# Loading all raw weights at once, splitting them ahead of the jobs, and moving three gathers and five loads

## The chip, the cores and the metric

The kernel runs on one core of one Trainium2 chip. The metric is the device time of one execution in microseconds. The kernel before took 1120.15 us (median of three runs, 1119.07 to 1122.03). The profiled execution took 1120.02 us, of which the profile's span covers 1118.3 us.

## The reference, cut to what matters

For each of 512 samples, 39 table rows of 16 values are gathered, giving x with shape (batch, 39, 16). Three layers (CIN layers) follow, and then a small tower:

```
e = stack([tbl_f[ids[:, f]] for f in 0..38], axis=1)       # (512, 39, 16)
prev = x = e
for k in 0, 1, 2:                                          # 39 or 128 rows in prev, 128 units out
    z = einsum('bmd,bhd->bdmh', x, prev)                   # outer product over fields
    t = einsum('bdc,co->bdo', z, w[k]) + b[k]              # w0: 39*39 x 128, w1, w2: 39*128 x 128
    t = transpose(t); t = t / sqrt(sum(t * t over units and d))
    logit.append(t); prev = t
features = sum(concatenate(logit), axis=-1)                # then dense_ctx, W_top1, W_top2, W_top3
```

All is float32. The raw weights w1 and w2 of layers 1 and 2 are 128 x 39 x 128 values each (2.5 MB).

## The kernel before

**Tiling.** The batch is cut into 16 chunks of 32 samples, 512 columns (sample, d) each. Layers 1 and 2 are computed as *jobs*: a job (k, c, q) is layer k, chunk c and one quarter (128 columns). An iteration `it` holds four jobs of layer 1 for chunk it, and then four jobs of layer 2 for chunk it - 1. So jobs 0 to 3 are layer 1 of chunk 0, jobs 4 to 7 layer 1 of chunk 1, jobs 8 to 11 layer 2 of chunk 0, and so on: 128 jobs.

**A job** has 10 banks of up to four fields. For each bank TensorE does three matmuls (lines 533 to 535): low part of prev by high weights, high prev by low weights, high by high. This is how float32 accuracy is had from the rounded f32r type; it needs each raw weight split in a high part (`split_high`, a copy on ScalarE, line 406) and a low part (`split_low`, a subtraction of two tiles in SBUF on VectorE, line 690). Five banks (`bank_a`, ring of two) are scaled by x on ScalarE (`scale_bank`, L423) and added up on GpSimd (`add_bank`, L307). The other five (`bank_d`, ring of three) are scaled and added on VectorE (`add_field`, L723), which begins when the four GpSimd adds of its job are done; `merge` (L742) folds the parts. TensorE takes D and A banks in turn (places 0 to 9 of a job), and its A banks run seven banks ahead of the job (LEAD). The last D bank of a job has three fields and so 384 columns, which marks the end of a job in the trace (place 8).

**Layer 0** of chunk c is done in pairs of fields. The gathered rows go through DRAM: GpSimd gathers chunk c in ten indirect DMAs (`gather`, L295) into one of two buffers; SyncE waits for them, stores them in `x_scratch` (`store_chunk`, L355 to 359), waits for the store and loads them back, copied and shifted, as `x_pairs` (`load_pairs`, L368 and L374; 14 DMAs in four groups p = 0 to 3). VectorE multiplies each group (`make_pairs`, L701, two tiles of SBUF in), TensorE sums tile by tile (`pair_matmul`, L598, 7 tiles). Then `finish` (L447, L450), `norms`, `roots`, `reciprocal_step`, `make_prev` (L788), `high` (L463, ScalarE) and `low` (L312, GpSimd) give the two parts of prev for the next layer.

**Order written out by hand.** Each engine executes one fixed list. GpSimd: the gathers of chunk 0, two constants (`ones`, `identity`), the gathers of chunk 1, `low(1, 0)`, the adds of seven banks, and then for each job its five adds with gathers of chunk it + 2 between them: three a job in iteration 0 (jobs 0 to 2, the tenth in job 3), two a job later. `start_chunk(c)` comes before the first gather of a chunk: it waits until chunk c - 1 has been gathered and chunk c - 2 stored, and makes the row numbers of chunk c + 1 (L280). VectorE has the pairs of chunk 2 at fields 2 and 12 of job 4, 12 of job 5 and 5 of job 6; TensorE sums the first tile after place 5 of job 4.

**The weights before.** ScalarE's queue loads w0a and w0b, the biases, and then w1 in three parts, each of which is issued when the one before has landed (L471 to 473). They are split at once, before the pairs of chunk 0. The raw w2 comes in six parts (`W2_PARTS`): the first is loaded after chunk 0's pairs, and in each of jobs 0 to 5 ScalarE splits one and issues the next (L489 to 494), and VectorE splits its low part behind field 18 (L834). The low w2 is wanted by the first layer 2 bank, seven banks ahead of job 8.

Of the kernel before, what the change touches and what calls it, by code (L numbers as in the profile page):

```python
# [123 lines left out]
W2_PARTS = [(0, 7), (7, 14), (14, 21), (21, 27), (27, 33), (33, 39)]  # L124
W1_PARTS = [(0, 16), (16, 28), (28, 39)]
# [5 lines left out]
def cin_kernel(nc, idx_in, base_in, table, ctx_t, w0a, w0b, w1, w2, b0, b1, b2,  # L131
# [7 lines left out]
    with ExitStack() as ctx:  # L139
# [73 lines left out]
        w_loaded = {k: sem(f"w{k}_loaded") for k in (1, 2)}  # L213
# [47 lines left out]
        def x_of(c, q, m):  # L261
            return x_col[:, c % 3, q, m:m + 1]

# [14 lines left out]
        def _(pool):  # L278
# [48 lines left out]
            for j in range(GATHERS):  # L327
                gather(1, j)
            low(1, 0)
            for at in range(LEAD):  # L330
                add_bank(at)
            for n in range(NJ):
                k, c, q = JOBS[n]
                it, place = (c, q) if k == 1 else (c + 1, q + TILES)

                per_step = 3 if it == 0 else 2
                first = place * per_step if it + 2 < CHUNKS else GATHERS
                if it + 2 < CHUNKS and place == 0:
                    start_chunk(it + 2)
                for a in range(A_BANKS):  # L340
                    add_bank(A_BANKS * n + LEAD + a)
                    if 1 <= a <= per_step and first + a - 1 < GATHERS:
                        gather(it + 2, first + a - 1)
                    for item, at in HALVES_AT.items():
                        if at == (n, a):
                            low(*item)

        @block.sync
        def _(sp):
# [12 lines left out]
            def load_pairs(c, p):  # L362
                rows = scratch[c, :, :].rearrange("(m b) e -> m (b e)", b=CB)
                tiles = PAIR_GROUPS[p]
                for kk in range(PER_TILE):
                    at = slice(kk * FIELDS, (kk + 1) * FIELDS)
                    if p == 0:
                        sp.dma_start(x_rep[at, :], rows[0:FIELDS, :]).then_inc(pairs_loaded[p], 16)  # L368
                    offsets = [PAIR_OFFSETS[PER_TILE * i + kk] for i in tiles if PER_TILE * i + kk < OFFSETS]
                    if offsets:  # L370
                        first = rows[offsets[0]:offsets[0] + FIELDS, :]
                        window = bass.AP(first.tensor, first.offset,
                                         [[ROWS, FIELDS], [PER_TILE * ROWS, len(offsets)], [1, ROWS]])
                        sp.dma_start(x_rot[at, tiles[0]:tiles[0] + len(offsets), :],  # L374
                                     window).then_inc(pairs_loaded[p], 16)

# [3 lines left out]
            for c in range(CHUNKS):  # L380
# [4 lines left out]
                for p in range(NP):  # L385
                    load_pairs(c, p)
                if c + 1 < CHUNKS:
                    store_chunk(c + 1)
                if c == 2:

                    sp.wait_ge(w_lo_made[1], len(W1_PARTS))
                    sp.wait_ge(w_lo_made[2], len(W2_PARTS))
# [10 lines left out]
        def _(act):  # L403
            def split_high(k, part, lo, hi):
                act.wait_ge(w_loaded[k], 16 * (part + 1))
                nc.scalar.activation(w_hi[k][:, lo:hi, :], w_raw[k][:, lo:hi, :], ACT.Copy).then_inc(w_hi_made[k], 1)
# [58 lines left out]

            act.dma_start(w0_sb[0:PAIR_ROWS, :, :], w0a).then_inc(w0_loaded, 16)
# [13 lines left out]
            act.dma_start(w_raw[2][:, 0:W2_PARTS[0][1], :], w2[:, 0:W2_PARTS[0][1], :]).then_inc(w_loaded[2], 16)  # L480
# [44 lines left out]
        def _(pe):  # L525
# [11 lines left out]
            def bank_for_act(at):  # L537
# [4 lines left out]
                if n == 0:  # L542
                    m = a * PER_BANK
                    pe.wait_ge(w_lo_made[1], 1 + sum(m >= lo for lo, _ in W1_PARTS[1:]))
                if (k, c, q) == (2, 0, 0) and a == 0:
                    pe.wait_ge(w_lo_made[2], len(W2_PARTS))
# [6 lines left out]
            def bank_for_dve(n, d):  # L553
                k, c, q = JOBS[n]
                at = D_BANKS * n + d
                if n == 0:
                    pe.wait_ge(w_lo_made[1], len(W1_PARTS))
# [129 lines left out]
        def _(dve):  # L687
            def split_low(k, part, lo, hi):
                dve.wait_ge(w_hi_made[k], part + 1)
# [118 lines left out]
            features(0)  # L808
            for n in range(NJ):
                for u in range(D_FIELDS):  # L810
# [23 lines left out]
                    if u == 18 and n < len(W2_PARTS):  # L834
                        split_low(2, n, *W2_PARTS[n])
# [65 lines left out]
```

## Time and profile before

| | |
|---|---|
| median of three runs | 1120.15 us |
| profiled execution, its span | 1120.02 us, 1118.3 us |
| TensorE (PE) busy | 1049.8 us, 94% |
| VectorE (DVE) busy | 939.6 us, 84% |
| GpSimd (POOL) busy | 900.5 us, 81% |
| ScalarE (ACT) busy | 814.0 us, 73% |
| mean granted TensorE clock | 0.989 |
| moved by DMA | 41.18 MB |

Times are microseconds from the start of the span. An engine's busy share is over the whole span, so it says nothing on a single stage: stages are read from the timeline (what ran when), the windows (busy time, clock and DMA in a stretch) and the chain of waits (what the end of the program hung on, step by step). SP is SyncE, which only issues DMAs; SPq and ACTq are DMA issues of those engines. "issue" is time in which an engine waited for nothing that the profile shows.

### The profile page before, as it was taken

The page shows a single profiled execution, that of the slowest core. Times are in us where ns is not written, and L with a number is a line of the kernel's source. Part 1 is how long each engine was busy: PE and PEld are TensorE (multiplying, and loading weights), DVE is VectorE, ACT ScalarE, POOL GpSimd, SP SyncE. Part 2 cuts the span into 40 slices and gives each one's busy share as a digit, 9 for nine tenths or more (in the row PEclk, how much of TensorE's full clock was granted, in tenths as well). Part 3 has the DMA queues.
Part 4 walks back from the last instruction along what each step waited for, and adds up shares of the span by engine and source line. Part 5 has one row for each costly group of instructions (what it writes and reads, how often), then busy time and mean ns, then how long its engine had stood idle before and what let it go on. Part 6 is the DMA issues. An engine that isn't in the chain of part 4 may idle for free.

```text
span 1118.3 us, 17869 instructions
## 1 busy us (share of the span) xinstructions
PE 1049.8 (94%) x4376; PEld 788.5 (71%) x4376; DVE 939.6 (84%) x3189; ACT 814.0 (73%) x2756; POOL 900.5 (81%) x726
## 2 busy tenths in 40 slices
PE   0696999999999999999999999999999999999999
PEld 0364677777777777777777777777777777778773
DVE  2285789899889989899998989999898998898892
ACT  2464587877878787787868777786878778788872
POOL 6586698888989888888988888888888888677770
PEclk9898999999999999999999999999999999999999
DMA  5513022020203002030302102020300203000000
GB/s 157 131 48 100 2 74 51 7 68 3 71 3 72 3 7 67 3 71 3 72 3 46 29 4 71 3 71 3 66 8 8 66 3 72 1 1 1 1 1 0
DMA packets 57166, 41.18 MB, mean 37 GB/s; under 512 B 37963, under 2 KB 40907, under 8 KB 56934
## 3 DMA queue, kind: packets, MB, share of 16 engines
q1 hardware_dynamic: 49522, 32.81, 12.2%
q10 hardware_dynamic: 2420, 5.96, 1.7%
q0 software_dynamic: 5120, 1.29, 1.5%
q8 instruction: 34, 0.56, 0.2%
q14 instruction: 70, 0.57, 0.2%
HBM read 38.09 MB, written 1.94 MB: 36 GB/s over the span
## 4 chain that ended last, share of the span: by engine, by line
PE 58%; POOL 26%; ACT 7%; issue 5%; DMA 2%; DVE 1%; SPq 1%; POOLq 0%; ACTq 0%; DVEq 0%
POOL sums L307 20%; PE acc L598 9%; PE bank_a L533 9%; PE bank_a L535 8%; PE bank_a L534 8%; PE bank_d L533 7%; PE bank_d L535 7%; PE bank_d L534 7%; POOL gathered L295 5%; ACT scaled L423 5%; ACT t L447 1%; DMA x_pairs<-x_scratch 1%; ACT squares L450 1%; PE turned L574 1%; PE bank_a L652 1%
## 5 line engine op out<-in xcount | busy, mean ns | idle before, releaser
L307 POOL TENSOR_TENSOR sums<-sums,scaled 128x512 f32<-128x512 f32 x512 | 686.7, 1342 | 141.8 <-ACT scaled L423 107.3
L723 DVE SCALAR_TENSOR_TENSOR sums<-bank_d,x_col,sums 128x128 f32<-128x128 f32 x2176 | 626.5, 339 | 108.8 <-PE bank_d L535 66.4
L423 ACT ACTIVATE scaled<-bank_a,x_col 128x128 f32<-128x128 f32 x2048 | 585.9, 382 | 153.0 <-PE bank_a L535 146.4
L533 PE MATMUL bank_a<-w_hi,prev_lo 128*128 128x512 f32 x640 | 283.1, 442 | 21.1 <-ACT scaled L423 8.9
L533 PE MATMUL bank_d<-w_hi,prev_lo 128*128 128x512 f32 (+1 forms) x640 | 278.0, 434 | 5.5 <-DVE sums L742 5.4
L535 PE MATMUL bank_a<-w_hi,prev_hi 128*128 128x512 f32 x640 | 254.4, 398 | 0.0
L534 PE MATMUL bank_a<-w_lo,prev_hi 128*128 128x512 f32 x640 | 253.8, 396 | 0.0
L535 PE MATMUL bank_d<-w_hi,prev_hi 128*128 128x512 f32 (+1 forms) x640 | 245.6, 384 | 0.0
L534 PE MATMUL bank_d<-w_lo,prev_hi 128*128 128x512 f32 (+1 forms) x640 | 245.4, 383 | 0.0
L423 ACT ACTIVATE sums<-bank_a,x_col 128x128 f32<-128x128 f32 x512 | 146.7, 372 | 70.5 <-PE bank_a L535 70.5
L295 POOL DMA_INDIRECT gathered<-in_table,idx x160 | 169.4, 1059 | 30.9 <-issue 19.2
L533 PEld LDWEIGHTS bank_a<-w_hi,prev_lo 128*128 128x128 f32 x640 | 121.1, 189 | 71.2 <-ACT scaled L423 23.6
L533 PEld LDWEIGHTS bank_d<-w_hi,prev_lo 128*128 128x128 f32 x640 | 121.0, 189 | 54.2 <-DVE sums L723 12.3
L534 PEld LDWEIGHTS bank_a<-w_lo,prev_hi 128*128 128x128 f32 x640 | 121.6, 190 | 33.4 <-issue 13.7
L534 PEld LDWEIGHTS bank_d<-w_lo,prev_hi 128*128 128x128 f32 x640 | 121.4, 190 | 30.2 <-issue 11.1
L535 PEld LDWEIGHTS bank_a<-w_hi,prev_hi 128*128 128x128 f32 x640 | 121.2, 189 | 29.1
L535 PEld LDWEIGHTS bank_d<-w_hi,prev_hi 128*128 128x128 f32 x640 | 120.6, 188 | 22.2
L598 PE MATMUL acc<-z,w_sb 117*128 117x512 f32 (+1 forms) x224 | 116.2, 606 | 7.6 <-DVE z L701 7.0
L701 DVE TENSOR_TENSOR z<-x_pairs 117x1024 f32<-117x1024 f32 x64 | 101.9, 1594 | 14.4 <-DMA x_pairs<-x_scratch 14.4
L723 DVE SCALAR_TENSOR_TENSOR bank_d<-bank_d,x_col,sums 128x128 f32<-128x128 f32 x256 | 78.0, 348 | 10.2 <-PE bank_d L535 8.2
L742 DVE TENSOR_TENSOR sums<-bank_d,sums 128x128 f32<-128x128 f32 x256 | 71.2, 278 | 0.0
L598 PEld LDWEIGHTS acc<-z,w_sb 117*128 117x128 f32 (+1 forms) x224 | 42.1, 195 | 20.3 <-issue 13.5
(57 smaller groups left out, 470.5 us busy)
## 6 DMA issues: line engine op xcount, KB each, us to landing
x_pairs<-x_scratch SPq DMA_DIRECT2D x144, 156.0 KB
x_pairs<-x_scratch SPq DMA_DIRECT2D x80, 78.0 KB
gathered<-in_table,idx POOLq DMA_INDIRECT x160
w_raw<-in_w ACTq DMA_DIRECT2D x3, 448.0 KB
x_scratch<-gathered SPq DMA_DIRECT2D x16, 72.0 KB, 2.2
w_raw<-in_w ACTq DMA_DIRECT2D x3, 384.0 KB
w_raw<-in_w ACTq DMA_DIRECT2D x1, 1024.0 KB
w_raw<-in_w ACTq DMA_DIRECT2D x1, 768.0 KB
```

The costliest lines, as they stand in the source:

```text
L295: nc.gpsimd.indirect_dma_start(out=gathered[0:n, c % 2, j, :], out_offset=None, in_=table[:, :], in_offset=bass.IndirectOffsetOnAxis(ap=id ...
L307: nc.gpsimd.tensor_tensor(out=sums[:, n % SUMS, :, :], in0=sums[:, n % SUMS, :, :], in1=scaled[:, a - 1, :, :], op=ALU.add).then_inc(a_add ...
L423: op = nc.scalar.activation(to[:, i, :], bank_a[at % A_RING][:, i * UNITS:(i + 1) * UNITS], ACT.Copy, scale=x_of(c, q, a * PER_BANK + i))
L447: nc.scalar.activation(t[:, k, :], ps[:, :], ACT.Identity, bias=bias[:, k:k + 1]).then_inc(biased, 1)
L450: nc.scalar.activation(squares[:, :], ps[:, :], ACT.Square, bias=bias[:, k:k + 1]).then_inc(squared, 1)
L533: nc.tensor.matmul(to, lo, w_h, start=True, stop=False)
L534: nc.tensor.matmul(to, hi, w_l, start=False, stop=False)
L535: return nc.tensor.matmul(to, hi, w_h, start=False, stop=True)
L598: mm = nc.tensor.matmul(acc0[:, :], w0_sb[0:rows, tile, :], z0[0:rows, tile, :], start=(tile == 0), stop=(tile == PAIR_TILES - 1))
L701: nc.vector.tensor_tensor(out=z0[0:rows, tiles[0]:tiles[0] + count, :], in0=x_rep[0:rows, :].unsqueeze(1).to_broadcast([rows, count, ROWS] ...
L723: nc.vector.scalar_tensor_tensor(out=taken(n, u) if u in LEFT else total, in0=taken(n, u), scalar=x_of(c, q, A_FIELDS + u), in1=total, op0 ...
L742: nc.vector.tensor_tensor(out=out, in0=in0, in1=in1, op=ALU.add).then_inc(merged, 1)
```

## The change

`W_LOADS` are three DMAs a layer; `W_PIECES` are the parts in which they are split, as before. ScalarE's queue now issues w1 (three DMAs) ahead of w0a and w0b, then the biases, then w2 (three DMAs) and the small ones of the tower, with no wait between. ScalarE splits all of w1 and three pieces of w2, waits for the store of chunk 0, issues the pair loads of groups 1 and 3 of chunk 0 itself (SyncE issues groups 0 and 2), and splits the other three pieces. VectorE waits for `ones`, so until GpSimd has issued chunk 0's gathers, splits w1 and three pieces of w2, makes chunk 0's pairs, splits piece 3, does the norm of chunk 0, waits for `low(1, 0)` and splits pieces 4 and 5. The splits in jobs 0 to 5 are gone. GpSimd starts chunk 2 ahead of `low(1, 0)`: row numbers and three gathers; the seven others are three a job in jobs 0 and 1 and one in job 2.

```diff
-W2_PARTS = [(0, 7), (7, 14), (14, 21), (21, 27), (27, 33), (33, 39)]
-W1_PARTS = [(0, 16), (16, 28), (28, 39)]
+W_LOADS = {1: [(0, 16), (16, 28), (28, 39)], 2: [(0, 14), (14, 27), (27, 39)]}
+W_PIECES = {1: [(0, 16), (16, 28), (28, 39)], 2: [(0, 7), (7, 14), (14, 21), (21, 27), (27, 33), (33, 39)]}
+GATHERS_BEFORE = 3
+W2_FIRST, W2_SECOND = 3, 4
+SP_GROUPS, ACT_GROUPS = [0, 2], [1, 3]
...
             for j in range(GATHERS):
                 gather(1, j)
+            start_chunk(2)
+            for j in range(GATHERS_BEFORE):
+                gather(2, j)
             low(1, 0)
...
                 first = place * per_step if it + 2 < CHUNKS else GATHERS
-                if it + 2 < CHUNKS and place == 0:
+                if it == 0:
+                    first += GATHERS_BEFORE
+                elif it + 2 < CHUNKS and place == 0:
                     start_chunk(it + 2)
...
-                for p in range(NP):
-                    load_pairs(c, p)
+                for p in range(NP) if c else SP_GROUPS:
+                    load_pairs(sp, c, p)
...
+            def load_raw(k):
+                for part, (lo, hi) in enumerate(W_LOADS[k]):
+                    act.dma_start(w_raw[k][:, lo:hi, :], raws[k][:, lo:hi, :]).then_inc(w_loaded[k][part], 16)
+
+            load_raw(1)
             act.dma_start(w0_sb[0:PAIR_ROWS, :, :], w0a).then_inc(w0_loaded, 16)
             act.dma_start(w0b_sb[0:PAIR_ROWS, :, :], w0b).then_inc(w0_loaded, 16)
             for k, b in enumerate((b0, b1, b2)):
                 act.dma_start(bias[:, k:k + 1], b).then_inc(bias_loaded, 16)
-            for part, (lo, hi) in enumerate(W1_PARTS):
-                if part:
-                    act.wait_ge(w_loaded[1], 16 * part)
-                act.dma_start(w_raw[1][:, lo:hi, :], w1[:, lo:hi, :]).then_inc(w_loaded[1], 16)
-            for part, (lo, hi) in enumerate(W1_PARTS):
-                split_high(1, part, lo, hi)
-            act.wait_ge(pairs_loaded[NP - 1], PAIR_LOADS[NP - 1] * 16)
+            load_raw(2)
             act.dma_start(top3_sb[:, :], w_top3).then_inc(top_bias_loaded, 16)
...
-            act.dma_start(w_raw[2][:, 0:W2_PARTS[0][1], :], w2[:, 0:W2_PARTS[0][1], :]).then_inc(w_loaded[2], 16)
+            for piece in range(len(W_PIECES[1])):
+                split_high(1, piece)
+            for piece in range(W2_FIRST):
+                split_high(2, piece)
+            act.wait_ge(scratch_stored, 48)
+            for p in ACT_GROUPS:
+                load_pairs(act, 0, p)
+            for piece in range(W2_FIRST, len(W_PIECES[2])):
+                split_high(2, piece)
...
             for n in range(NJ):
-                if n < len(W2_PARTS):
-                    lo, hi = W2_PARTS[n]
-                    split_high(2, n, lo, hi)
-                    if n + 1 < len(W2_PARTS):
-                        lo, hi = W2_PARTS[n + 1]
-                        act.dma_start(w_raw[2][:, lo:hi, :], w2[:, lo:hi, :]).then_inc(w_loaded[2], 16)
...
-            for part, (lo, hi) in enumerate(W1_PARTS):
-                split_low(1, part, lo, hi)
+            dve.wait_ge(ones_made, 1)
+            for piece in range(len(W_PIECES[1])):
+                split_low(1, piece)
+            for piece in range(W2_FIRST):
+                split_low(2, piece)
             for p in range(NP):
                 make_pairs(0, p)
+            for piece in range(W2_FIRST, W2_SECOND):
+                split_low(2, piece)
             sum_values(0, 0)
...
             features(0)
+            dve.wait_ge(prev_lo_made[1], 1)
+            for piece in range(W2_SECOND, len(W_PIECES[2])):
+                split_low(2, piece)
             for n in range(NJ):
...
-                    if u == 18 and n < len(W2_PARTS):
-                        split_low(2, n, *W2_PARTS[n])
```

## Rows read from the trace of the kernel before

**Rows 1.** The page: shares of the chain of waits, by engine.
```profile
PE 58%; POOL 26%; ACT 7%; issue 5%; DMA 2%; DVE 1%; SPq 1%; POOLq 0%; ACTq 0%; DVEq 0%
```

**Rows 2.** Timeline of TensorE, 384-column banks: jobs 3, 4, 11, 12, 20.
```profile
91.45 0.34 PE L533 MATMUL bank_d<-w_hi,prev_lo 128*128 128x384 f32 x1
...
113.55 0.34 PE L533 MATMUL bank_d<-w_hi,prev_lo 128*128 128x384 f32 x1
...
173.70 0.34 PE L533 MATMUL bank_d<-w_hi,prev_lo 128*128 128x384 f32 x1
...
181.48 0.34 PE L533 MATMUL bank_d<-w_hi,prev_lo 128*128 128x384 f32 x1
...
245.55 0.34 PE L533 MATMUL bank_d<-w_hi,prev_lo 128*128 128x384 f32 x1
```

**Rows 3.** Chain of waits around 100 us: start, length, what.
```profile
96.64 2.38 DMA gathered<-in_table,idx
...
100.10 1.92 DMA x_scratch<-gathered
...
104.04 4.26 DMA x_pairs<-x_scratch
...
109.70 2.05 PE acc L598 x2
```

**Rows 4.** Chain of waits from the start to the first job.
```profile
1.28 4.22 DMA base_sb<-in_bases
...
17.64 2.74 DMA gathered<-in_table,idx
...
25.45 3.65 DMA x_pairs<-x_scratch
...
30.93 7.96 PE acc L598 x14
...
44.24 1.27 POOL prev_lo L312
```

**Rows 5.** Timeline of GpSimd: row numbers, gathers of chunks 1 and 2.
```profile
20.46 1.51 POOL L280 TENSOR_TENSOR idx<-ids_sb,base_sb 128x10 int32<-128x10 int32 x1 [1.30 <-DMA gathered<-in_table,idx]
22.14 2.34 POOL L295 DMA_INDIRECT gathered<-in_table,idx  x1 [0.17 <-issue]
...
37.29 0.92 POOL L295 DMA_INDIRECT gathered<-in_table,idx  x1 [0.30 <-issue]
...
84.67 0.96 POOL L295 DMA_INDIRECT gathered<-in_table,idx  x1
...
90.82 0.96 POOL L295 DMA_INDIRECT gathered<-in_table,idx  x1 [2.07 <-issue]
```

**Rows 6.** Timeline of VectorE: splits of w1, its first add, splits in jobs.
```profile
19.61 5.50 DVE L690 TENSOR_TENSOR w_lo<-w_raw,w_hi 128x2048 fp32r<-128x2048 f32 x3 [12.19 <-ACT w_hi L406]
...
55.74 0.61 DVE L723 SCALAR_TENSOR_TENSOR sums<-bank_d,x_col,sums 128x128 f32<-128x128 f32 x2 [12.13 <-POOL sums L307]
...
66.80 1.07 DVE L690 TENSOR_TENSOR w_lo<-w_raw,w_hi 128x896 fp32r<-128x896 f32 x1
...
93.35 2.01 DVE L690 TENSOR_TENSOR w_lo<-w_raw,w_hi 128x768 fp32r<-128x768 f32 x1
```

**Rows 7.** Windows: last three columns are TensorE clock, DMA share, GB/s.
```profile
8.00:10.00 2.00, 0.00 (x0) 0.00 (x0) 0.00 (x0) 0.00 (x0) 1.55 (x2) 1.00 0.80 329
...
28.00:30.00 2.00, 0.32 (x4) 0.35 (x4) 0.43 (x1) 0.00 (x0) 1.39 (x3) 1.00 0.95 209
...
134.00:138.00 4.00, 4.00 (x12) 2.87 (x12) 1.26 (x5) 1.14 (x4) 1.72 (x2) 0.65 0.03 2
```

**Rows 8.** Chain of waits in job 6.
```profile
131.39 2.25 issue
133.64 0.76 PE bank_a L533
```

More of the change, by code:

```diff
@@ L212, in cin_kernel @@
         bias_loaded = sem("bias_loaded")
-        w_loaded = {k: sem(f"w{k}_loaded") for k in (1, 2)}
+        w_loaded = {k: [sem(f"w{k}_loaded{part}") for part in range(len(W_LOADS[k]))] for k in (1, 2)}
         w_hi_made = {k: sem(f"w{k}_hi_made") for k in (1, 2)}
@@ L262, in x_of, with load_pairs @@
             return x_col[:, c % 3, q, m:m + 1]
+        def load_pairs(queue, c, p):
+            rows = scratch[c, :, :].rearrange("(m b) e -> m (b e)", b=CB)
+            tiles = PAIR_GROUPS[p]
+            for kk in range(PER_TILE):
+                at = slice(kk * FIELDS, (kk + 1) * FIELDS)
+                if p == 0:
+                    queue.dma_start(x_rep[at, :], rows[0:FIELDS, :]).then_inc(pairs_loaded[p], 16)
+                offsets = [PAIR_OFFSETS[PER_TILE * i + kk] for i in tiles if PER_TILE * i + kk < OFFSETS]
+                if offsets:
+                    first = rows[offsets[0]:offsets[0] + FIELDS, :]
+                    window = bass.AP(first.tensor, first.offset,
+                                     [[ROWS, FIELDS], [PER_TILE * ROWS, len(offsets)], [1, ROWS]])
+                    queue.dma_start(x_rot[at, tiles[0]:tiles[0] + len(offsets), :],
+                                    window).then_inc(pairs_loaded[p], 16)
         def bdim(ap):
@@ L360, in store_chunk @@
                              g[:, 0:5, :]).then_inc(scratch_stored, 16)
[L362 to L375, printed above, removed]
             sp.dma_start(ids_sb[:, :], idx_in).then_inc(ids_loaded, 16)
@@ L389, in _ @@
                 if c == 2:
-                    sp.wait_ge(w_lo_made[1], len(W1_PARTS))
-                    sp.wait_ge(w_lo_made[2], len(W2_PARTS))
+                    sp.wait_ge(w_lo_made[1], len(W_PIECES[1]))
+                    sp.wait_ge(w_lo_made[2], len(W_PIECES[2]))
                     sp.dma_start(top1c_sb, w_top1[3 * 128:3 * 128 + EMB, :]).then_inc(top_loaded, 16)
@@ L403, in _, with split_high @@
         def _(act):
-            def split_high(k, part, lo, hi):
-                act.wait_ge(w_loaded[k], 16 * (part + 1))
+            def split_high(k, piece):
+                lo, hi = W_PIECES[k][piece]
+                part = [first <= lo < last for first, last in W_LOADS[k]].index(True)
+                act.wait_ge(w_loaded[k][part], 16)
                 nc.scalar.activation(w_hi[k][:, lo:hi, :], w_raw[k][:, lo:hi, :], ACT.Copy).then_inc(w_hi_made[k], 1)
@@ L543, in bank_for_act @@
                     m = a * PER_BANK
-                    pe.wait_ge(w_lo_made[1], 1 + sum(m >= lo for lo, _ in W1_PARTS[1:]))
+                    pe.wait_ge(w_lo_made[1], 1 + sum(m >= lo for lo, _ in W_PIECES[1][1:]))
                 if (k, c, q) == (2, 0, 0) and a == 0:
-                    pe.wait_ge(w_lo_made[2], len(W2_PARTS))
+                    pe.wait_ge(w_lo_made[2], len(W_PIECES[2]))
                 if q == 0 and a == 0:
@@ L687, in _, with split_low @@
         def _(dve):
-            def split_low(k, part, lo, hi):
-                dve.wait_ge(w_hi_made[k], part + 1)
+            def split_low(k, piece):
+                lo, hi = W_PIECES[k][piece]
+                dve.wait_ge(w_hi_made[k], piece + 1)
                 nc.vector.tensor_tensor(out=w_lo[k][:, lo:hi, :], in0=w_raw[k][:, lo:hi, :],
```

3 lines of the change are left out of this document (2 added, 1 removed).

## The prediction

> **What bounds the kernel now.** I read first the page's chain: its end hangs on TensorE for 58% and on GpSimd for 26% [rows 1], so over most of the span matmuls and adds hand over to each other. The change touches none of that. The 384-column banks on TensorE's timeline mark the jobs: from job 12 to job 20 they are 245.55 - 181.48 = 64.07 us apart [rows 2], and the same distance repeats, with one of 64.8, to the end. What is gained or lost ahead of job 12 should stand unchanged in the total, so I look only at the first 180 us.
>
> Two things there are longer than in the repeating part. From job 3 to job 4 the banks are 113.55 - 91.45 = 22.1 us apart, where the like step from job 11 to job 12 takes 7.78 [rows 2]. From job 4 to job 12 it is 67.93 us, 3.9 more than 64.07. The chain of waits says what the first gap is: the tenth gather of chunk 2, its landing, the store, the load of the first pairs, and the matmuls behind them [rows 3]. The second is in job 6, where TensorE waits 2.25 us for the low part of layer 2's first prev and then runs slowly [rows 8]. The chain from the start to the first job [rows 4] is the third place: 44 us in which row numbers, chunk 0's gathers, store, loads, 14 matmuls and the norm follow each other. There a delay counts in full.
>
> **Part 1: three gathers ahead of the first job (chunk 2 ready earlier).** The last gather of chunk 2 moves from job 3 (96.64 us) to the place in job 2 that now holds its seventh (84.67) [rows 3, 5]. Ahead of this place nothing is removed from GpSimd's list but one making of row numbers, at a time when TensorE is the bound; only some collision with VectorE's splits goes, some 0.3 us. So it is issued at 84.4 on the old clock. From the issue of the last gather to TensorE's first pair matmul it takes 109.70 - 96.64 = 13.1 us now [rows 3]: TensorE would have it at 97.5. When does TensorE want it? Job 3's last bank is at 91.45; I take 0.5 us off, for the VectorE splits and the gathers that no longer stand in jobs 2 and 3 (a split of 2.01 us at 93.35 [rows 6], and three gathers, one of them with 2.07 us idle ahead of it [rows 5], in the stretch where GpSimd was the bound). TensorE then comes to place 5 of job 4 at about 96.4 and waits 1.1 us. Job 4's last bank: 91.45 - 0.5 + 7.8 + 1.1 = 99.85, against 113.55: **-13.7 us**. Bounds: without any wait 14.8; if GpSimd reaches the gather 3 us later than I think, because it becomes the bound in jobs 0 and 1, 10.7.
>
> **Part 2: the splits leave jobs 0 to 5.** On VectorE six of 1.07 to 2.01 us [rows 6], on ScalarE six. In jobs 0 to 3 they lie beside TensorE or GpSimd and are in part 1. In job 5 one of about 1 us stands ahead of the norm of layer 1's first chunk, on which TensorE waits in job 6. Without it prev and its low part come about 0.7 us sooner, so the wait of 2.25 [rows 8] becomes 1.5. After this wait the granted clock falls (0.65 over 134 to 138 us, a mix of the two levels 1.2 and 2.4 GHz [rows 7]), and the first matmul takes 0.76 [rows 8]. If the clock holds after the shorter wait, the missing 0.35 of 4 us come back, 1.4. I count 0.7 and half of 1.4: **-1.4 us**; bounds -0.3 and -3.
>
> **Part 3: w1 first in the queue (row numbers later).** The ids and bases wait now 4.22 us for landing [rows 4], with w0 being loaded beside them. After the change 1 MB of w1 goes first, in rows of 8 KB for 3.5 KB, and w2 behind it. The trace doesn't show a small load beside so large rows. Lower bound 0 (the small rows are first in a queue of their own); upper bound: the wait doubles, 4.2. The nearest row is the last gather of chunk 0, which lands 2.74 after its start with w1's third part in flight, against 2.38 with nearly nothing [rows 4, 3]: small packets beside bulk lose 0.4 a time. Two loads in a row: I take **+1.0**, range 0 to 4.
>
> In all 5.96 MB now stand in one queue. At the 329 GB/s of 8 to 10 us [rows 7] they are in after 18 us, near 20 us, before the store; at 209 GB/s [rows 7] after 28.5 us, near 30, in the middle of the pair loads. I take the first, as its rows are the weights' own.
>
> w0 is now behind w1, so its two additions on VectorE fall among chunk 0's gathers: **+0.2**. The rest of VectorE's work waits for `ones`.
>
> **Part 4: two queues for chunk 0's pairs.** TensorE's 14 matmuls run from 30.93 for 7.96 us with no hole [rows 4]: they hang on group 0 alone, and what groups 1 and 3 gain is worth nothing. But the DMA engines are 95% busy from 28 to 30 us [rows 7], and group 0 (three loads of 78 KB, three of 156 KB, 0.7 MB) now shares them with 0.47 MB of group 1, issued beside it. At 209 GB/s that is 2.2 us if group 1 were all in front, and 0 if its loads fill holes of the issue. I take a third: **+0.7**, range -0.3 to 2.2. The Trainium skill, "DMA: Bandwidth & Descriptors", section "Issuing engines are not separate DMA queues", speaks against this part as well: DMAs of several issuers run on the same 16 engines, and only issue time is saved. By it the part brings nothing where the load is bound by the engines; if issue were the bound (six issues ahead of the landing in [rows 4]), it would neither help nor harm group 0.
>
> **Part 5: GpSimd ahead of the first job.** VectorE's splits lengthen GpSimd's instructions. While w1 was split (19.61 to 25.11 [rows 6]) the making of row numbers took 1.51 and a gather 2.34, where a gather alone takes 0.92 [rows 5]. With the short 1.15 of the next gather the loss was about 2.9 us in 4.65 us of overlap, 0.6 us a us. Now the splits run from about 18.8 for 5.5 + 3 x 1.07 = 8.7 us, to 27.5: 2.4 us more overlap, +1.5 us. Piece 3, in the last gathers, gives +0.6. Chunk 1's last gather then starts at 37.29 + 2.1 = 39.4, and lands 2.3 later, at 41.7. Only then may chunk 2 start: 0.4 for row numbers and start, three gathers at 1.25 with the 0.30 between them, 3.8: about 46.0. `low(1, 0)`, which started at 44.24 with its input ready [rows 4], stands behind them in GpSimd's list, and TensorE's first job waits for it. That is 1.8 late, of which 0.7 is already in part 4 (the gathers don't wait for the pairs): **+1.1**. Bounds: 0 if the overlap costs nothing more, 3.5 if each us of VectorE's splits costs a full one. The two pieces that VectorE splits behind `low` fit in the 12.13 us that it idles before the first job's adds [rows 6].
>
> For the overlap the Trainium skill has a rule: "SBUF — State Buffer", section "Who interferes with whom", says that a tensor_tensor with both inputs in SBUF and a GpSimd instruction that reads SBUF exclude each other, the second waiting for the whole first one. By that each split would cost its full length where GpSimd has work, and part 5 would be about +2.5 for +1.1. The rows show 0.6, as GpSimd can slip in between two splits.
>
> **Sum.** -13.7 - 1.4 + 1.0 + 0.2 + 0.7 + 1.1 = -12.1 us. The profiled execution took 1120.02, the median of the runs is 1120.15, so both are the same base: 1120.1 - 12.1 = 1108.0.
>
> **Rivals.**
> *A, the start eats more of it.* The bulk loads run at 209 GB/s and last to 30 us. Chunk 0's pair loads and w2's last 1.5 MB share the engines (+4 for group 0), ScalarE gets to its pair loads only when 5.2 MB are in, so groups 1 and 3 are late (+1), ids lose 2 to 3. For it: the only row with the DMA engines full shows 209 GB/s. Against: that row is of 2 KB pieces, the one with 329 of weights [rows 7]. Time: 1108.0 + 7 = 1115.0.
> *B, the gap closes wholly and the start costs nothing.* Ids, groups and `low` as before, no wait in job 4, clock kept in job 6: -14.8 - 2.1 - 0.3 = 17.2 less, 1102.9. For it: each of the costs is in parts not shown by the trace. Against: GpSimd's list must be 1.8 us longer by rows.
> *C, the gap is there all the same.* Chunk 2's loads wait for something else than the tenth gather. SyncE's list for it has only the pairs and the transpose of chunk 1, made in job 0. With the gap left and the start worse by 3: 1123; with the gap half closed, 1116. Against: the chain names each step [rows 3].
> *D, slower: the repeating part gets longer.* With another distance between the engines at job 12, the hand-over of matmuls and adds could settle on a longer period. It has one place and one price: with 13.5 iterations to go, 64.07 must become over 65.0 to eat 12 us; with 65.3 the time is 1124. For it: TensorE and GpSimd share the chain, so a shift between them can matter. Against: the period in the trace is reached after a start with a hole of over 10 us, so it doesn't look as if it hung on the start.
>
> **Chances.** The forecast (1104.5 to 1111.5) 0.66, A 0.14, B 0.10, C 0.05 (half of it slower), D 0.05, of which most is slower. I expect to tell 0.3%, 3.4 us, from no change. Faster: forecast, A, B and a little of C, 0.92; same: 0.03; slower: 0.05. The range for 8 in 10: 1103.0 to 1114.0, which takes in half of A and of B.
>
> **What the profile after would show.** Right: the 384-column bank of job 4 about 8.5 us behind that of job 3; the tenth gather of chunk 2 near 87 us; `low(1, 0)` starting near 47, right behind a gather; ids landing 1 us later; the wait in job 6 at or under 1.5 us, and 64.07 us between jobs 12 and 20. Wrong: group 0's first product before 29.6 (part 4 has the wrong sign), w2 in flight beyond 25 us (A), over 3 us of wait for pairs in job 4 (part 1), a period other than 64.07 (D). The forecast fails most easily at the start: the three unseen costs there sum to 2.9, and could be 0 or 8.

## The result, and the profile after

The changed kernel takes 1113.95 us (median of six runs, 1113.52 to 1115.38), the kernel before beside it 1120.91: ratio 0.994, 95% interval 0.9928 to 0.9953. The forecast was 12.1 us less; it became 7.0 by the medians (6.7 by the ratio). The direction was right and the size little more than half; 1113.95 is at the upper end of the range of 1103.0 to 1114.0. The two profiled spans differ by 1118.3 - 1112.3 = 6.0 us, and the ledger below is made for them.

First TensorE's timeline, the 384-column banks of jobs 0 to 4, 12 and 20, which answer to [rows 2]:

```profile
69.90 0.74 PE L550 MATMUL bank_d<-w_hi,prev_lo 128*128 128x384 f32 x1
80.58 0.34 PE L550 MATMUL bank_d<-w_hi,prev_lo 128*128 128x384 f32 x1
91.80 0.53 PE L550 MATMUL bank_d<-w_hi,prev_lo 128*128 128x384 f32 x1
100.22 0.34 PE L550 MATMUL bank_d<-w_hi,prev_lo 128*128 128x384 f32 x1
107.98 0.34 PE L550 MATMUL bank_d<-w_hi,prev_lo 128*128 128x384 f32 x1
...
175.76 0.34 PE L550 MATMUL bank_d<-w_hi,prev_lo 128*128 128x384 f32 x1
...
239.78 0.34 PE L550 MATMUL bank_d<-w_hi,prev_lo 128*128 128x384 f32 x1
```

The gap is gone: from job 3 to job 4 are 7.76 us for 22.1, and the repeating part is unchanged (239.78 - 175.76 = 64.02 for 64.07). But job 3 ends 8.77 us later than before (100.22 for 91.45), where I had expected 2.5. Job by job the lateness is 6.2 us in jobs 0 and 1 (their banks stood at 63.73 and 74.43 before), 7.7 in job 2 and 8.8 in job 3. Job 2 before the change, with the wait ahead of it:

```profile
83.34 0.50 PE L533 MATMUL bank_a<-w_hi,prev_lo 128*128 128x512 f32 x1 [1.87 <-POOL prev_lo L312]
...
84.14 0.35 PE L533 MATMUL bank_d<-w_hi,prev_lo 128*128 128x384 f32 x1
```

The chain from the start shows where the 6.2 come from; it answers to [rows 4]:

```profile
23.59 0.39 SPq L382
...
24.66 1.94 DMA x_scratch<-gathered
...
28.65 7.05 DMA x_pairs<-x_scratch
...
37.09 7.97 PE acc L615 x14
...
50.40 1.27 POOL prev_lo L334
```

The store of chunk 0 is issued at 23.59, where it was at 20.40 before: 3.2 late. The last load of group 0 takes 7.05 for 3.65 us, and the first pair matmul comes at 37.09 for 30.93, 6.16 late. From there on to `low(1, 0)` (50.40 for 44.24) nothing is added: the early gathers end before it. GpSimd's timeline, which answers to [rows 5], says when row numbers and gathers came:

```profile
8.87 0.48 POOL L302 TENSOR_TENSOR idx<-ids_sb,base_sb 128x10 int32<-128x10 int32 x2 [8.35 <-DMA base_sb<-in_bases]
...
47.23 0.94 POOL L317 DMA_INDIRECT gathered<-in_table,idx  x1 [0.30 <-issue]
50.40 1.26 POOL L334 TENSOR_TENSOR prev_lo<-prev,prev_hi 128x512 fp32r<-128x512 f32 x1 [2.22 <-ACT prev_hi L477]
...
86.04 0.96 POOL L317 DMA_INDIRECT gathered<-in_table,idx  x1 [2.13 <-issue]
87.02 2.67 POOL L329 TENSOR_TENSOR sums<-sums,scaled 128x512 f32<-128x512 f32 x2
89.65 1.26 POOL L334 TENSOR_TENSOR prev_lo<-prev,prev_hi 128x512 fp32r<-128x512 f32 x1
...
92.30 0.92 POOL L317 DMA_INDIRECT gathered<-in_table,idx  x1
```

The bases land at 8.8 and not at 5.5 us. In job 1 the ninth gather of chunk 2 (the program's 29th) has 2.13 us of idle ahead of it, and behind it in the list stands `low(1, 1)`, the low part for chunk 1, which TensorE wants in job 2 already, as its A banks run seven ahead. This idle was in the old trace too, at the same gather [rows 5], but there it was in job 2, with `low(1, 1)` already done. TensorE's timeline and the windows (last columns: granted clock, DMA share, GB/s) show what follows:

```profile
90.97 0.50 PE L550 MATMUL bank_a<-w_hi,prev_lo 128*128 128x512 f32 x1 [4.00 <-POOL prev_lo L334]
```

```profile
4.00:6.00 2.00, 0.00 (x0) 0.00 (x0) 0.00 (x0) 0.00 (x0) 0.00 (x0) 1.00 1.03 418
6.00:8.00 2.00, 0.00 (x0) 0.00 (x0) 0.00 (x0) 0.00 (x0) 0.00 (x0) 1.00 0.99 399
...
34.00:36.00 2.00, 0.17 (x2) 0.20 (x3) 0.28 (x1) 0.00 (x0) 1.39 (x3) 1.00 0.88 195
...
92.00:96.00 4.00, 4.00 (x13) 3.37 (x13) 1.82 (x8) 2.28 (x8) 2.87 (x4) 0.61 0.13 13
129.00:131.00 2.00, 2.00 (x5) 0.96 (x4) 1.26 (x5) 0.91 (x4) 0.96 (x1) 0.57 0.05 4
```

TensorE waits 4.00 us for that low part, where it waited 1.87 before. Over 92 to 96 us, behind this wait, the granted clock is 0.61, a mix of 2.4 and 1.2 GHz: some 3 us of it are at the lower level. The raw weights fill the DMA engines from 4 to 12 us, with up to 418 GB/s, and are in by about 21 us.

The ledger, in us of the profiled executions: start +6.2, jobs 2 and 3 +2.6, gap -14.3, job 4 to job 12 -0.15, the rest -0.3, sum -6.0. The forecast had, in the same places, +3.0, -0.5, -13.2, -1.4 and 0.

### The profile page after: what moved, and what is told of

The parts are those of the page before. It is cut to its first block, busy times and chain, and to the rows that moved or that the text cites. A ratio compares the mean times of both kernels' runs of the same rounds, so it can differ in the third digit from the quotient of the medians.

```text
span 1112.3 us, 17868 instructions
## 1 busy us (share of the span) xinstructions
PE 1047.5 (94%) x4376; PEld 788.4 (71%) x4376; DVE 939.0 (84%) x3189; ACT 812.8 (73%) x2756; POOL 900.9 (81%) x726
## 3 DMA queue, kind: packets, MB, share of 16 engines
q1 hardware_dynamic: 49145, 32.17, 12.1%
## 4 chain that ended last, share of the span: by engine, by line
PE 58%; POOL 27%; issue 7%; ACT 7%; DMA 1%; DVE 1%; SPq 0%; POOLq 0%; ACTq 0%; DVEq 0%
POOL sums L329 22%; PE acc L615 9%; PE bank_a L550 9%; PE bank_a L552 8%; PE bank_a L551 8%; PE bank_d L550 7%; PE bank_d L551 7%; PE bank_d L552 7%; POOL gathered L317 5%; ACT scaled L437 5%; ACT t L461 1%; PE turned L591 1%; PE bank_a L669 1%; DMA x_pairs<-x_scratch 1%; ACT squares L464 1%
## 5 line engine op out<-in xcount | busy, mean ns | idle before, releaser
L317 POOL DMA_INDIRECT gathered<-in_table,idx x160 | 168.7, 1054 | 31.3 <-issue 19.6
```

The costliest lines, as they stand in the source:

```text
L317: nc.gpsimd.indirect_dma_start(out=gathered[0:n, c % 2, j, :], out_offset=None, in_=table[:, :], in_offset=bass.IndirectOffsetOnAxis(ap=id ...
```

## The experiments

Theory: three things cost what the gap gave. (1) The 6 MB of bulk in one queue delay whatever is small and on the chain: ids, then the landing of chunk 0's gathers. (2) Group 0 of the pair loads shares the DMA engines with groups 1 and 3. (3) Gathers moved forward stand ahead of `low(1, 1)`. The rival to each stands in the expectation. All ratios are against the kernel before on the same chip. The kernels did not all run on one chip, and the kernel before took between 1120.9 and 1121.7 us beside them, so two kernels of the table are compared by their ratios; where the intervals overlap, as those of one_queue and the changed kernel just do, the difference of the times alone does not tell.

| kernel | median us | ratio (95% interval) |
|---|---|---|
| changed | 1113.95 | 0.994 (0.9928 to 0.9953) |
| one_queue | 1112.01 | 0.9914 (0.9898 to 0.9931) |
| ids_first | 1113.45 | 0.9926 (0.9908 to 0.9945) |
| no_early_gathers | 1125.74 | 1.0037 (1.0024 to 1.005) |
| before_gathers | 1112.03 | 0.9913 (0.9896 to 0.9929) |
| three_two_two | 1114.2 | 0.9933 (0.9917 to 0.995) |
| w2_behind | 1108.01 | 0.9879 (0.9862 to 0.9895) |
| before_gathers_ids | 1112.41 | 0.992 (0.9903 to 0.9936) |
| w0_first | 1114.03 (one run) | |
| behind_low | 1111.09 | 0.9912 (0.9897 to 0.9928) |
| six_early | 1107.4 | 0.9872 (0.9857 to 0.9887) |
| w2_behind_chunk1 | 1106.09 | 0.9859 (0.9844 to 0.9874) |
| all_moved | 1102.93 | 0.9832 (0.9819 to 0.9845) |

**The gap: no_early_gathers and before_gathers.**

```diff
-GATHERS_BEFORE = 3
+GATHERS_BEFORE = 0
```

> All ten gathers of chunk 2 are in the jobs again (three, three, three, one); the row numbers are still made ahead of the first job. Theory (the gap in job 4 hangs on the tenth gather): the step from the last bank of job 3 to that of job 4 goes from 7.76 back to about 22, jobs 2 and 3 lose their 2.6 us of delay, time 1114 + 14.3 - 2.6 = 1125.5, so slower than before the change. Rival (the removed splits closed the gap): the step stays under 12 and the time under 1118.

Jobs 3 and 4 on TensorE's timeline of this kernel:

```profile
97.30 0.34 PE L550 MATMUL bank_d<-w_hi,prev_lo 128*128 128x384 f32 x1
118.78 0.52 PE L550 MATMUL bank_d<-w_hi,prev_lo 128*128 128x384 f32 x1
```

The gap is back (21.48 us), and the time is 1125.74, slower than before the change. So the removed splits did not close it, and all of the change but the three gathers is a loss of 0.4%, with the interval clear of 1. Jobs 2 and 3 take 16.3 us here for 19.6 in the changed kernel: their delay comes with the gathers too. The 29th gather has its idle here as well (2.26 us), but behind `low(1, 1)`.

The other way round, the gathers alone in the kernel before:

```diff
                 gather(1, j)
+            start_chunk(2)
+            for j in range(3):
+                gather(2, j)
             low(1, 0)
...
-                if it + 2 < CHUNKS and place == 0:
+                if it == 0:
+                    first += 3
+                elif it + 2 < CHUNKS and place == 0:
                     start_chunk(it + 2)
```

> The kernel before the change with only the gathers moved (three of chunk 2 ahead of the first job, seven in jobs 0 to 2); weights, splits and queues as before. Theory (the gathers alone close the gap, all else of the change costs about 6 us at the start): first job at 45.7 to 46.5 as before, gap gone but for 1 us, time 1107 to 1110, faster than the changed kernel. Rival (the splits in the jobs keep VectorE or GpSimd late, so that gap is only half closed): 1112 or more.

```profile
96.72 0.34 PE L538 MATMUL bank_d<-w_hi,prev_lo 128*128 128x384 f32 x1
104.49 0.35 PE L538 MATMUL bank_d<-w_hi,prev_lo 128*128 128x384 f32 x1
114.15 0.42 PE L538 MATMUL bank_d<-w_hi,prev_lo 128*128 128x384 f32 x1
127.01 0.52 PE L538 MATMUL bank_d<-w_hi,prev_lo 128*128 128x384 f32 x1
```

The gap is closed (7.77 us from job 3 to 4), and the kernel is some 2 us faster than the changed one (the intervals touch), but not at 1107 to 1110. It came out where the rival had put it, but not for the rival's reason: the gap is closed whole. Its first job starts at 47.31, for 45.65 before and 51.81 in the changed kernel; 1.4 of these 1.7 us are in the 14 pair matmuls, which took 9.34 us here for 7.96, and nothing in this edit touches them. Job 3 ends 96.72 - 91.45 = 5.3 us later than before, 3.9 of it in jobs 2 and 3: the loss there comes with the gathers, not with the weights. From job 5 to job 6 it takes 12.86 us, where the kernels without splits in jobs 4 and 5 mostly take 10.94. From job 4 to job 12 it is 69.37 us, for 67.78 in the changed kernel and 66.27 in one_queue: with the gathers moved, removing the splits is worth 1.6 to 3.1 us.

**Group 0: one_queue.**

```diff
-SP_GROUPS, ACT_GROUPS = [0, 2], [1, 3]
+SP_GROUPS, ACT_GROUPS = [0, 1, 2, 3], []
```

> SyncE issues all four groups of chunk 0's pair loads again; all else as in the changed kernel. Theory (two queues share the DMA engines, so group 0 ends with group 1 and 3): the last load of group 0 lands about 3.6 us after its issue and not 7.05, the first pair matmul comes 3.4 us earlier (33.7 for 37.09), and the time falls by 1 to 3.4 us; less than 3.4 if GpSimd's early gathers, which end at 48.17, then hold up low(1, 0) (its input would be ready at 46.9). Rival (the loads are slow at that moment for another reason, such as the split of the weights or bulk in flight): landing stays near 7 us and the time near 1114.

VectorE's first product of pairs, here and (second fence) in the changed kernel:

```profile
32.40 1.23 DVE L719 TENSOR_TENSOR z<-x_pairs 117x1024 f32<-117x1024 f32 x1 [1.53 <-DMA x_pairs<-x_scratch]
34.99 1.22 DVE L719 TENSOR_TENSOR z<-x_pairs 117x1024 f32<-117x1024 f32 x1 [1.36 <-DMA x_pairs<-x_scratch]
```

```profile
35.72 4.20 DVE L719 TENSOR_TENSOR z<-x_pairs 117x1024 f32<-117x1024 f32 x4 [4.91 <-DMA x_pairs<-x_scratch]
```

Group 0 comes 3.3 us earlier with one queue; with two, all four products run back to back, so groups 1 to 3 landed at its heels, and the DMA engines were through at 37 us (share 0.77 over 36 to 37, 0.03 over 37 to 38). In one_queue they were through at about 37 us too. At the 192 to 241 GB/s of the stretch from 28 to 36 us the 0.64 MB on the second queue are 2.7 to 3.3 us, most of the 3.4. The first job gains 2.8 (49.04 for 51.81), as TensorE's 14 pair matmuls took 8.5 us here for 8.0. The three early gathers ended at 47.45, and `low(1, 0)` started at 47.64, when its input was there: it did not wait for them.

The profiled span is 3.5 us shorter than the changed kernel's, and 1.6 of that is not the queues' doing. In job 6 TensorE waits 1.97 us in both kernels. Here the granted clock (third column from the right) holds behind it, where in the changed kernel it fell to 0.57:

```profile
127.00:129.00 2.00, 2.00 (x9) 1.40 (x8) 1.13 (x5) 1.04 (x5) 0.60 (x1) 1.00 0.05 4
129.00:131.00 2.00, 2.00 (x12) 1.41 (x11) 1.81 (x7) 1.75 (x8) 1.28 (x1) 1.00 0.00 0
```

The step from job 6 to job 7 is 8.36 us here and 9.93 there.

**Ids and bulk: ids_first, w0_first, before_gathers_ids, w2_behind.**

```diff
+            act.wait_ge(ids_loaded, 32)
             load_raw(1)
```

> ScalarE waits until ids and bases have landed before it issues the raw weights. Theory (the two small loads queue behind rows of w1 on the same engines): bases land 3 us or less after issue for 7.5 now, the first gather starts at or before 6.24, all up to job 0 is 3.3 us or more earlier, time 1110 to 1111; the weights then end near 25 us and may collide with the store, which would give back 1. Rival (the first DMAs of a program are slow by themselves): landing stays over 6 us and nothing is gained.

The landing of the bases on the chain, and GpSimd's next row numbers, which wait for the last gather of chunk 0:

```profile
1.28 1.67 DMA base_sb<-in_bases
```

```profile
15.09 0.92 POOL L317 DMA_INDIRECT gathered<-in_table,idx  x1 [0.30 <-issue]
...
21.73 4.12 POOL L302 TENSOR_TENSOR idx<-ids_sb,base_sb 128x10 int32<-128x10 int32 x1 [4.49 <-DMA gathered<-in_table,idx]
```

My theory was half right. The bases land in 1.67 us for 7.5, and the gathers start 5.9 us earlier. But the last one, begun at 15.09, has landed only at 21.7, 6.6 us later for 2.6. It lands as the bulk ends: the DMA engines are 96% busy over 18 to 20 us here. The store gains 1.9 us of 5.9. One of these reaches TensorE (first pair matmul at 36.13 for 37.09), and there the 14 pair matmuls took 9.4 us for 8.0, so the first job is not earlier (52.29 for 51.81). The time is the same as the changed kernel's within what can be told.

```diff
-            load_raw(1)
             act.dma_start(w0_sb[0:PAIR_ROWS, :, :], w0a).then_inc(w0_loaded, 16)
             act.dma_start(w0b_sb[0:PAIR_ROWS, :, :], w0b).then_inc(w0_loaded, 16)
+            load_raw(1)
```

> The changed kernel with w0a and w0b ahead of w1 in the queue; no other edit. Theory (what the small loads wait for is bytes already queued on their engines, whatever the rows): bases land in 6 to 7.5 us, not 4.2, for w1 follows w0 with no pause now. Rival (the order of w0 and w1 made the difference, 8 KB rows for 3.5 KB): back to 4.2 to 4.5. One look at the profile.

```profile
1.28 4.27 DMA base_sb<-in_bases
```

```profile
17.79 0.92 POOL L317 DMA_INDIRECT gathered<-in_table,idx  x1 [0.30 <-issue]
...
23.07 1.55 POOL L302 TENSOR_TENSOR idx<-ids_sb,base_sb 128x10 int32<-128x10 int32 x1 [1.66 <-DMA gathered<-in_table,idx]
```

Here the rival was right: with w0 in front the bases land in 4.27, as before, though w1 follows at once. What stands at the head of the queue counts for them. (The time is that of one run.) The store is issued at 23.02 all the same, 0.6 us ahead of the changed kernel's 23.59, as the last gather lands 5.2 us after its start for 2.6: again the bulk takes back what the bases gave.

```diff
+            act.wait_ge(ids_loaded, 32)
             act.dma_start(w0_sb[0:PAIR_ROWS, :, :], w0a).then_inc(w0_loaded, 16)
```

(on top of before_gathers)

> The kernel before with the early gathers (before_gathers, 1112.0), and ScalarE waits for the ids before it issues w0. Theory: with the throttled weights as only bulk the whole gain of the early ids stays: bases land in 1.7 us for 4.6, first job 2.5 to 3 us earlier (44.5 for 47.3), time 1109 to 1109.5. Rival (the landing of chunk 0's gathers hangs on bulk here as well): less than 1 us is left.

```profile
1.28 1.87 DMA base_sb<-in_bases
...
15.28 3.80 DMA gathered<-in_table,idx
...
20.21 4.27 DMA x_scratch<-gathered
```

A miss, and the rival held: even the loads of w1 that are issued one after another, moved 2 us later, fall beside the last gather (3.80 for 2.35 in before_gathers) and the store (4.27 for 1.92). First job at 47.45 for 47.31.

Then w2 away from chunk 0's gathers. On top of one_queue and the wait for ids (VectorE's splits move alike):

```diff
-            load_raw(2)
             act.dma_start(top3_sb[:, :], w_top3).then_inc(top_bias_loaded, 16)
...
-            for piece in range(W2_FIRST):
-                split_high(2, piece)
-            act.wait_ge(scratch_stored, 48)
...
-            for piece in range(W2_FIRST, len(W_PIECES[2])):
-                split_high(2, piece)
+            act.wait_ge(pairs_loaded[NP - 1], PAIR_LOADS[NP - 1] * 16)
+            load_raw(2)
...
             high(1, 0)
+            for piece in range(W2_FIRST):
+                split_high(2, piece)
...
+                if n < 3:
+                    split_high(2, W2_FIRST + n)
```

> Ids before all bulk, one queue for chunk 0's pairs, w1 at once, w2's three loads behind the pair loads of chunk 0 instead of beside its gathers; ScalarE splits three pieces of w2 ahead of the first job and three in jobs 0 to 2, VectorE the same. Theory (chunk 0's gathers can't land before the bulk is through, which took all the gain of the early ids in ids_first): last gather of chunk 0 lands near 18 us for 21.7, store near 18, first pair matmul near 28.4, first job near 43.5 for 52.3 in ids_first and 49.0 in one_queue, time 1105 to 1108. Rival (w2 has no part in it): first job at 46 or later and the time at 1109 or more.

```profile
17.42 0.39 SPq L382 DMA_DIRECT2D x_scratch<-gathered  x1
```

```profile
35.81 4.78 DMA gathered<-in_table,idx
...
44.53 1.28 POOL prev_lo L334
```

The store is issued at 17.42 (6.2 us earlier than in the changed kernel), the first pair matmul at 27.86. That is the theory; and the kernel is 4 us under one_queue. Half of the start's gain is lost once more: w2 now falls on the last gather of chunk 1, which lands 4.78 us after its start, and `low(1, 0)` stands behind the start of chunk 2. The first job is at 45.94, not at 43.5.

**Jobs 2 and 3: three_two_two, behind_low, six_early.** All on top of one_queue.

```diff
-                per_step = 3 if it == 0 else 2
+                per_step = (3, 2, 2, 0)[place] if it == 0 else 2
...
-                    first += GATHERS_BEFORE
+                    first = (3, 6, 8, 10)[place]
```

> On top of one_queue (1112.0, step from job 1 to job 2 11.94 us, from 2 to 3 8.65): chunk 2's seven gathers in the jobs are three, two, two instead of three, three, one, so that the ninth and tenth stand behind low(1, 1) in GpSimd's list. Theory (an idle of about 2.2 us belongs to the 29th gather of the program; ahead of low(1, 1) it makes TensorE wait 4 us and drop its clock, which is where jobs 2 and 3 lost 2.6 to 3.3 us): the idle moves behind low(1, 1), TensorE's wait ahead of it is under 2 us, the two steps are 9.4 and 7 to 8; but the tenth gather comes late and the step to job 4 grows by up to 4. Time 1109 to 1113. Rival (the low part waits for something else, such as the adds): the step to job 2 stays over 11.

TensorE's wait ahead of the banks of chunk 1:

```profile
85.57 0.50 PE L550 MATMUL bank_a<-w_hi,prev_lo 128*128 128x512 f32 x1 [0.99 <-POOL prev_lo L334]
```

0.99 us for 4.11 in one_queue; the steps to jobs 2 and 3 are 8.17 and 6.92 for 11.94 and 8.65. The place of the ninth gather is the cause: in one_queue it had 2.22 us of idle and 0.96 us of its own ahead of `low(1, 1)`, which are the 3.1 us. The tenth now came later in the job, and the step to job 4 took 14.84: 7.1 back for 5.5 won. The idle did not move behind `low(1, 1)`; with 6.4 us between the starts of the 28th and 29th gathers there was none.

```diff
-            for j in range(GATHERS_BEFORE):
-                gather(2, j)
             low(1, 0)
+            for j in range(0, 3):
+                gather(2, j)
```

> On top of one_queue: the three early gathers of chunk 2 stand behind low(1, 0) in GpSimd's list instead of ahead of it. Theory (in one_queue low(1, 0) is 0.7 us late behind them, and GpSimd idles 4.3 us after it, in which three gathers of 1.25 us fit): low starts 0.7 us earlier, the first add is not later, time 0.5 to 0.7 under one_queue (1112.0), about what can be told. Rival (VectorE's two splits behind low lengthen these gathers past the 4.3 us): first add up to 1 us late, no gain.

No gain that can be told, and the premise was false for one_queue: `low` was ready to run 0.2 us after the gathers had ended, so nothing stood in its way that could be taken off. Here it started at 48.31, as the pair matmuls ended later, and the first job at 49.72. What the run does show is that three gathers fit behind `low`: from the first job's start to its 384-column bank are 17.7 us, for 17.4 in one_queue.

```diff
             for j in range(GATHERS_BEFORE):
                 gather(2, j)
             low(1, 0)
+            for j in range(3, 6):
+                gather(2, j)
...
+                per_step = (3, 0, 1, 0)[place] if it == 0 else 2
...
+                    first = (6, 9, 9, 10)[place]
```

> On top of one_queue: six gathers of chunk 2 ahead of the first job (three ahead of low(1, 0), three behind), three in job 0, none in job 1, one in job 2. Theory (jobs 2 and 3 lost time because low(1, 1) stands behind job 1's three gathers and the 2.2 us idle of the 29th): TensorE's wait for low(1, 1) falls from 4.1 to under 1 us, the steps to jobs 2 and 3 go from 11.94 and 8.65 to about 8.2 and 7, and the tenth gather is no later than in one_queue (88.99), so the step to job 4 is at most 10. Time 1108 to 1110. Rival (GpSimd as a whole is the bound there, wherever its gathers stand): TensorE waits elsewhere, time at 1111 or more.

```profile
72.48 0.96 POOL L317 DMA_INDIRECT gathered<-in_table,idx  x1 [2.15 <-issue]
```

```profile
84.69 0.50 PE L552 MATMUL bank_a<-w_hi,prev_lo 128*128 128x512 f32 x1 [0.29 <-POOL prev_lo L334]
```

The idle of the 29th gather is now in job 0, where TensorE is the bound and it costs nothing. TensorE's wait is 0.29, the steps to jobs 2, 3 and 4 are 7.48, 6.92 and 8.94, and the time is 4.6 us under one_queue, although its clock fell in job 6, where that of one_queue held. GpSimd as a whole was not the bound; the order of its list was.

**Both together: w2_behind_chunk1 and all_moved.** The first is w2_behind with the loads of w2 in a later place. Shown are the lines that stand there against the changed kernel; the wait for the pairs with w2's loads behind it, of w2_behind, is gone.

```diff
             roots(0)
+            act.wait_ge(gather_done, 2 * 16 * GATHERS)
+            load_raw(2)
             high(1, 0)
+            for piece in range(2):
+                split_high(2, piece)
...
+                if n < 4:
+                    split_high(2, 2 + n)
```

> w2_behind (1108.0) with w2's loads behind the landing of chunk 1's gathers too; two pieces split ahead of the first job, four in jobs 0 to 3. Theory (in w2_behind the last gather of chunk 1 lands 4.78 us after its start, beside w2, and start_chunk(2) and low(1, 0) behind it hold up the first job by some 3 us): landing 2.5, low(1, 0) at 41.7 to 42.5 for 44.53, first job at 43.3 to 44, time 1105 to 1106.5. Rival (w2 now meets chunk 1's pair loads, and these or the splits come late in job 0): no gain, or 1 us lost.

```profile
35.88 0.92 POOL L317 DMA_INDIRECT gathered<-in_table,idx  x1 [0.30 <-issue]
38.32 0.20 POOL L302 TENSOR_TENSOR idx<-ids_sb,base_sb 128x10 int32<-128x10 int32 x1 [1.52 <-DMA gathered<-in_table,idx]
...
42.17 1.27 POOL L334 TENSOR_TENSOR prev_lo<-prev,prev_hi 128x512 fp32r<-128x512 f32 x1
```

The last gather of chunk 1 lands 2.4 us after its start, `low(1, 0)` starts at 42.17, the first job at 43.59, as expected; 1106.09, with a ratio 0.002 under w2_behind and overlapping intervals.

On top of it, GpSimd's list:

```diff
-            for j in range(GATHERS_BEFORE):
+            for j in range(2):
                 gather(2, j)
             low(1, 0)
+            for j in range(2, 5):
+                gather(2, j)
...
+                per_step = (3, 1, 1, 0)[place] if it == 0 else 2
...
+                    first = (5, 8, 9, 10)[place]
```

> w2_behind_chunk1 with two early gathers ahead of low(1, 0), three behind it, three in job 0, one in job 1, one in job 2. Both theories together: first job near 43.3, TensorE's wait for low(1, 1) under 2 us, steps to jobs 2 to 4 about 8.5, 7.3 and 8 to 10. Time 1101 to 1104. If the job 2 part is wrong it is at 1105 like the kernel above.

```profile
82.04 0.34 PE L551 MATMUL bank_d<-w_hi,prev_lo 128*128 128x384 f32 x1
88.96 0.34 PE L551 MATMUL bank_d<-w_hi,prev_lo 128*128 128x384 f32 x1
97.96 0.34 PE L551 MATMUL bank_d<-w_hi,prev_lo 128*128 128x384 f32 x1
```

Job 4 ends at 97.96, for 107.98 in the changed kernel and 113.55 before. 1102.93 us, ratio 0.9832 (0.9819 to 0.9845): faster than both kernels. Its first job starts at 43.85, and the steps to jobs 2, 3 and 4 are 8.28, 6.92 and 9.00.

## Why the prediction was right in its direction and too large

- *What bounds, and that only the first jobs matter*: right. The period is 64.02, and what stood at job 12 stood at the end (-5.7 and -6.0). Rival D fell.
- *Part 1, the gap*: the cause was right, and the closing came to 14.3 us for 13.2 in the step to job 4. But I took 0.5 us off for jobs 2 and 3, and they became 2.6 longer. The step that failed is "I take 0.5 us off, for the VectorE splits and the gathers that no longer stand in jobs 2 and 3": I asked when the tenth gather would come and not what comes behind the moved ones. I had the idle of 2.07 us in [rows 5], counted it as removed, and it moved one job forward, ahead of `low(1, 1)`, on which TensorE then waited 4.00 us for 1.87. three_two_two and six_early show it. The 1.1 us over the forecast in the closing is luck. The tenth gather came at 92.30 and not near 87, but TensorE came to job 4 late as well, so there was no wait. In six_early and all_moved, where jobs 2 and 3 are not late, the step is 8.94 and 9.00, close to the 8.9 that I had worked out with a wait of 1.1.
- *Part 2, the splits*: -1.4 forecast, -0.15 measured from job 4 to job 12. The wait in job 6 fell from 2.25 to 1.97 only, not to 1.5, and the clock was lowered all the same (0.57 over 129 to 131 us). I had counted half of its price, and it fell on the bad side. In one_queue, ids_first, w0_first, w2_behind and behind_low the same wait (1.97 to 1.99) left the clock at 1.00, and from job 4 to job 12 they took 66.2 to 66.3 us, 1.7 to 1.8 less than the kernel before. In no_early_gathers, three_two_two, six_early, w2_behind_chunk1 and all_moved it fell. What decides it stays open. The splits of jobs 4 and 5 cost more in a kernel that has early gathers as well, 1.6 to 3.1 (before_gathers).
- *Part 3, ids*: the term of 1.0 measured 3.3, within its range. The nearest row that I took, a gather beside w1's last part, was no measure for two loads behind a full queue. The total of the bulk, which I placed near 20 us, was right (up to 418 GB/s). What I didn't see is that it bounds the landing of the gathers too, so that gathers which start earlier give little: 1.9 of 5.9 us at the store in ids_first, 0.6 of 3.2 in w0_first. The +0.2 for w0's additions had no row behind it. Some 0.1 of it shows among the gathers (the first starts 3.3 us late, the last 3.4), and nothing of it at the store, which is 3.2 late.
- *Part 4, two queues*: 0.7 forecast; the landing grew by 3.4, the first pair matmul by 3.0 of its own. This is the worst-sized term of the start, beyond its range of 2.2: I counted only group 1 as competitor, but group 3 follows in ScalarE's queue, and the 0.64 MB of both at 209 GB/s are 3.1 us. The Trainium skill, "DMA: Bandwidth & Descriptors", section "Issuing engines are not separate DMA queues", had it: the transfers share the engines and interleave. The trace agrees: group 1's product runs right behind group 0's, and all groups were in by 37 us.
- *Part 5, low(1, 0)*: 1.1 forecast, 0 measured. The gathers ended at 48.2, 2.2 us ahead of its input, because parts 3 and 4 had made the main chain later. GpSimd's own list became 1.3 us longer up to chunk 1's last gather (41.91 - 37.29, less 3.3 for the ids), for 2.1. In one_queue, too, the gathers ended 0.2 us before `low`. In three_two_two (48.05), w2_behind (44.53) and w2_behind_chunk1 (42.17) it did stand directly behind the last early one, 0.8, 2.4 and 0.2 us after its input was there, so the mechanism was real where the pairs came in time.

So the forecast was 6 us too good: 3.1 in jobs 2 and 3, 3.2 in the start (parts 3 and 4 too small, part 5 too large) and 1.2 in part 2, less 1.1 in the closing of the gap and 0.3 behind job 12.

Rival A gave 1115 and was near in number. Its ids (2 to 3) and group 0 (4) were near the measured 3.3 and 3.4, but by another cause: the bulk was through at about 21 us, and not at 30, and it was groups 1 and 3 that held up group 0.

## What to carry to other kernels

A transfer with a late deadline that is issued early takes its bandwidth from the ones with an early deadline: place it behind them, by a wait on their semaphore. When an operation moves forward in an engine's list, look for every operation that it now stands ahead of, and who waits for that one. Sharing a set of loads between two queues made the first one later here (35.7 us for 32.4) and the last one hardly earlier (near 37 in both); with a consumer that begins on the first, that is a loss.

## What the hardware showed that I had not expected

- The 29th gather of the program starts 3.1 to 3.7 us after the 28th, with 2.1 to 2.5 us of idle ahead of it, wherever it stands (90.82 before, 86.04 after, 72.48 in six_early), and with no idle where 6.4 us or more lie between the two starts (three_two_two, all_moved). A smaller one (0.85 to 1.0 us) stands ahead of the 58th and 116th, before and after. Its cause stays open.
- The 14 pair matmuls of chunk 0 took 7.96 us before and after, 8.51 in one_queue and 9.3 to 9.4 in before_gathers, behind_low and ids_first, with the granted clock at 1.00 in the windows: four to seven of them at a distance of 0.85 us and the others at 0.43. What ends the slow part stays open. It moves the first job by up to 1.4 us, so a comparison of first jobs is no finer than that.
- A wait of 1.97 us on TensorE in job 6 was followed by a lowered clock (0.57), but only 1.5 us after work had resumed; in one_queue the same wait was not, and after the wait of 1.87 in job 2 of the kernel before the clock held too. Executions of one kernel may differ in it as well, which isn't shown step by step: those of all_moved spanned from 1099.4 us at a mean clock of 0.997 to 1102.6 at 0.992.
